# Inverse square roots on VectorE: one second-order and one third-order step in place of three Newton steps

## The chip, the cores and the metric

The kernel runs on one core of a Trainium2 chip. The metric is device time in microseconds (us), the median of three runs. Engine names are those of the profile: PE is TensorE's matmul, PEld its weight load, DVE is VectorE, ACT is ScalarE, POOL is GpSimd and SP is SyncE, which only issues DMAs here.

## The reference

The input x is 4 x 256 rows of 256 float32 numbers. Four layers are added to it in turn, each on a layernorm of x:

```
x = x + tanh(g_xattn[0]) * L0_xattn(layernorm(x), ctx, mask)   # attention, 16 heads; its output is layernormed
x = x + tanh(g_ffn[0])   * L0_ffn(layernorm(x))                # one shared and seven routed experts, top 3
x = x + tanh(g_xattn[1]) * L1_xattn(layernorm(x), ctx, ctx)    # mLSTM cell, 16 heads, each head layernormed
x = x + tanh(g_ffn[1])   * L1_ffn(layernorm(x))                # block-quantised gated FFN, 256 -> 1024 -> 256

_layernorm(x):            (x - m) / sqrt(var + 1e-5)           # over the 256 features
L0_xattn, last line:      (delta - mu) / sqrt(var + 1e-5) * ln_gamma + ln_beta
L1_xattn, each head:      (h - mu) * rsqrt(mean((h - mu)^2) + 1e-6)      # over the head's 16 features
```

## The kernel before, in words

The 1024 rows of x lie in SBUF as eight tiles of 128 rows. Most steps run once for each half, that is for four tiles (n = 0 or 1). One list, `plan`, made by `step_order`, holds the names of all steps; every engine walks through the same list and takes the steps that it has a part in. So the order on each engine is fixed, and the engines meet through semaphores.

The inverse square root is computed by DVE alone, in `inverse_root` (line 1186). It makes a first guess with integer arithmetic on the bits of the float (line 1190) and improves it by three Newton steps of three instructions each (lines 1193, 1195 and 1197). Every one of these ten instructions waits until the one before it has ended: `seq.wait()` waits for the engine's own counter `v_seq`, which each instruction added with `seq.add` raises.

It is called twelve times, with three callers:
- `ln_in(k)`, line 1199, for k = 0 to 7: the statistics of the layernorm of x ahead of each of the four layers, for each half. The operands have 4 columns, one for each tile. `ln_out(k)` then writes the normalised tiles to `tok` (line 1223), which PE transposes (`turn` or `xt`).
- `delta_in(n)`, line 1290: the same for the output of the first attention; 4 columns. `delta_out(n)` adds the result to x.
- `cell_mid(n)`, line 1513: one root for each row and head of the mLSTM cell; 64 columns (4 tiles x 16 heads), in rows of `hstat`, which lies in the memory called `arows` in the profile. `cell_out(n)` uses it.

In the plan the roots stand so: `ln_in(0)` and `ln_in(1)` with the loads and the first transposes; `delta_in(0)` and `ln_in(2)` at the end of the first half's attention; `delta_in(1)` and `ln_in(3)` between the instructions of experts 3 to 5; `ln_in(4)` beside expert 9; `cell_mid(0)` and `ln_in(6)` beside experts 14 and 15; `ln_in(5)` beside the start of the last layer; `cell_mid(1)` and `ln_in(7)` just before the second half of the last layer.

Three other DVE steps are spoken of below. `up` makes the experts' hidden tiles (line 1375), and `accumulate` adds an expert's output to x (line 1386). `quantise` cuts the last layer's operands to blocks; its instructions at lines 1548 and 1550 follow each other with no wait between them. On POOL, `w_split` takes the rounded part off an expert's weights (line 659), and `quantise` hands `mx_grid` to PE (line 584).

Of the kernel before, what the change touches and what calls it, by code (L numbers as in the profile page):

```python
# [36 lines left out]
P = 128  # L37
F32, F32R, BF16, U32, I32, F8 = (mybir.dt.float32, mybir.dt.float32r, mybir.dt.bfloat16, mybir.dt.uint32, mybir.dt.int32,
                                 mybir.dt.float8e4)
ALU = mybir.AluOpType  # L40
# [6 lines left out]
E50, EM50 = float(np.exp(50.0)), float(np.exp(-50.0))  # L47
EXP_BITS = 0x7F800000
FAR = -1e30


class Count:
# [182 lines left out]
def flamingo_layers(nc, a, out):  # L235
# [12 lines left out]
    TH = HALF // P  # L248
# [3 lines left out]
    with ExitStack() as ctx_:  # L252
        place = {}

        def sb(name, shape, dt=F32):
            place[name] = -(-nc.sbuf_base // 32) * 32
            return ctx_.enter_context(nc.sbuf_tensor(name, shape, dt))
# [70 lines left out]
        mv = sb("mv", [P, NT, 2])  # L328
        ve = sb("ve", [P, 8, TH])
        ri = sb("ri", [P, 8, TH])  # L330
        ru = sb("ru", [P, TH])
        dve_ = sb("dve_", [P, 2, TH])
        dri = sb("dri", [P, 2, TH])
        lg = sb("lg", [P, 8, TH, NE])
# [848 lines left out]
        def _(v):  # L1183
            seq = Count(v, s["v_seq"])

            def inverse_root(y, w, u):


                seq.wait()
                seq.add(v.tensor_scalar(y.bitcast(I32), w.bitcast(I32), -0.5, float(0x5F3759DF), ALU.mult, ALU.add))  # L1190
                for _ in range(3):
                    seq.wait()
                    seq.add(v.tensor_tensor(u, y, y, ALU.mult))
                    seq.wait()
                    seq.add(v.scalar_tensor_tensor(u, u, -0.5, w, ALU.mult, ALU.mult))
                    seq.wait()
                    seq.add(v.scalar_tensor_tensor(y, u, 1.5, y, ALU.add, ALU.mult))

            def ln_in(k):

                use, n = k // 2, k % 2
                if use == 0:
                    v.wait_ge(s[f"x_loaded{n}"], 16)
                elif use == 2:
                    v.wait_ge(s["x2_acc"], TH * (NE + 1) * (n + 1))
                i0 = TH * n
                for i in range(i0, i0 + TH):
                    m = seq.add(v.bn_stats(st[:, i, :], x[:, i, :]))  # L1208
                seq.wait(m)
                for i in range(i0, i0 + TH):  # L1210
                    m = seq.add(v.bn_aggr(mv[:, i, :], st[:, i, :]))
                seq.wait(m)
                seq.add(v.tensor_scalar(ve[:, k, :], mv[:, i0:i0 + TH, 1], LN_EPS, None, ALU.add))
                inverse_root(ri[:, k, :], ve[:, k, :], ru[:, :])

            def ln_out(k):
                use, n = k // 2, k % 2
# [72 lines left out]
            def delta_in(n):  # L1290
                i0 = TH * n
                v.wait_ge(s["wo_biased"], 2 * n + 2)
                for i in range(i0, i0 + TH):
                    seq.add(v.bn_stats(st[:, i, :], tok[:, i, :]))
                seq.wait()
                for i in range(i0, i0 + TH):
                    seq.add(v.bn_aggr(mv[:, i, :], st[:, i, :]))
                seq.wait()
                seq.add(v.tensor_scalar(dve_[:, n, :], mv[:, i0:i0 + TH, 1], rs2[:, 1:2], LN_EPS, ALU.mult, ALU.add))
                inverse_root(dri[:, n, :], dve_[:, n, :], ru[:, :])  # L1300
                seq.wait()
                seq.add(v.tensor_scalar(dri[:, n, :], dri[:, n, :], rs2[:, 0:1], None, ALU.mult))

# [209 lines left out]
            def cell_mid(n):  # L1513
                v.wait_ge(s["h_squared"], n + 1)
                seq.add(v.tensor_reduce(hstat[:, 2, n, :], mt[:, :, :].rearrange("p a (h v) -> p (a h) v", v=HD), AX.X, ALU.add))
                seq.wait()
                seq.add(v.tensor_scalar(hstat[:, 3, n, :], hstat[:, 2, n, :], 1.0 / HD, CELL_EPS, ALU.mult, ALU.add))
                inverse_root(hstat[:, 4, n, :], hstat[:, 3, n, :], hstat[:, 5, n, :])

            def cell_out(n):  # L1520
                v.wait_ge(s["h_scaled"], n + 1)
# [82 lines left out]
```

## Time and profile before

| | before |
|---|---|
| median of three runs | 513.97 us |
| the three runs | 513.65, 520.17, 513.97 us |
| span of the profiled execution, first to last instruction | 516.7 us |
| instructions in it | 6750 |
| busy: PE, DVE | 366.7 us (71%), 364.3 us (71%) |
| busy: PEld, ACT, POOL | 247.4, 191.3, 154.6 us |
| mean granted TensorE clock, share of full speed | 0.867 |

The profile is one execution, and it gives no time of its own besides the span. The span counts from the first to the last instruction that the profiler records, and is 2.7 us above the median of the runs. Busy times are sums over the whole span, in which stages with different limits follow one another. In a timeline each line has the start in us, the length in us, the engine, the line of the kernel and what is written from what; the bracket at its end is the idle time of the engine just before it and what ended that.

### The profile page before, as it was taken

The numbers are of one execution on the slowest core, as the hardware profiler recorded it, in microseconds if no ns is written. First come the engines' busy times: TensorE is split into PE (matmuls) and PEld (weight loads), VectorE is DVE, ScalarE is ACT, GpSimd is POOL, SyncE is SP. The second block draws the span as 40 slices with busy tenths as digits, with TensorE's granted clock in tenths as the row PEclk, the third lists the DMA queues.
The fourth block names the chain that finished last, engine by engine and source line by source line (L and its number), as shares of the span: only waits on it lengthen the run. The fifth ranks groups of instructions, "written<-read, shape, count | busy, mean of one in ns | idle before, by whom it ended". The sixth has DMA issues, their size and how long they took to land.

```text
span 516.7 us, 6750 instructions
## 1 busy us (share of the span) xinstructions
PE 366.7 (71%) x2192; PEld 247.4 (48%) x2192; DVE 364.3 (71%) x887; ACT 191.3 (37%) x336; POOL 154.6 (30%) x150
## 2 busy tenths in 40 slices
PE   4664965628998859795975788797686468660665
PEld 2342542405565648584853556565563235530333
DVE  3174875395653498988788656754998697789895
ACT  2333752222441412251334445453201658721231
POOL 5058058100002544554622541212601220030230
PEclk9796997756999998997998899998977879977685
DMA  8499999930111121330498491364100192000001
GB/s 193 134 139 167 148 189 262 266 52 0 42 27 35 62 82 29 94 120 3 119 187 175 92 165 59 59 105 87 18 0 1 47 150 30 2 1 0 20 11 51
DMA packets 47009, 44.20 MB, mean 86 GB/s; under 512 B 6304, under 2 KB 45952, under 8 KB 46976
## 3 DMA queue, kind: packets, MB, share of 16 engines
q1 hardware_dynamic: 44768, 40.53, 38.6%
q0 software_dynamic: 1152, 2.20, 1.8%
q10 hardware_dynamic: 1056, 1.05, 0.7%
q8 instruction: 18, 0.29, 0.3%
q14 instruction: 15, 0.12, 0.1%
HBM read 36.43 MB, written 7.34 MB: 85 GB/s over the span
## 4 chain that ended last, share of the span: by engine, by line
PE 36%; DVE 33%; issue 14%; ACT 7%; DMA 5%; POOL 3%; SPq 1%; DVEq 0%; ACTq 0%; POOLq 0%
PE bank L848 9%; PE bank L874 5%; PE bank L776 4%; DMA probs<-in_L_xattn_Wq 3%; PE bank L733 2%; DVE probs L1264 2%; DVE tok L1223 2%; PE bank L984 2%; PE bank L948 2%; DVE mxraw L1552 2%; DVE mam L1394 2%; DVE probs L1479 1%; PE bank L896 1%; PE bank L810 1%; DVE st L1208 1%
## 5 line engine op out<-in xcount | busy, mean ns | idle before, releaser
L874 PE MATMUL bank<-wexp,wT 128*128 128x256 f32 x192 | 56.1, 420 | 10.1 <-DVE x L1386 10.0
L848 PE MATMUL bank<-tok_r,probs_r 128*128 128x512 f32 x104 | 47.1, 453 | 10.2 <-DVE wT L1375 7.0
L1264 DVE TENSOR_SCALAR probs<-probs,hi 128x512 f32<-128x512 f32 x64 | 32.8, 564 | 28.8 <-ACT probs L1045 28.8
L1097 ACT ACTIVATE silu_sb<-bank 128x512 f32<-128x512 f32 x32 | 19.1, 598 | 86.2 <-PE bank L848 86.2
L659 POOL TENSOR_TENSOR wexp_r<-wexp,probs_r 128x1024 fp32r<-128x1024 f32 x13 | 31.3, 2405 | 58.6 <-ACT probs_r L1056 58.5
L874 PEld LDWEIGHTS bank<-wexp,wT 128*128 128x128 f32 x192 | 38.4, 211 | 17.6 <-issue 12.4
L1045 ACT ACTIVATE probs<-bank 128x1024 f32<-128x1024 f32 x32 | 32.3, 1027 | 38.2 <-PE bank L760 38.2
L584 POOL TENSOR_TENSOR mx_grid<-parts,bl 128x1024 bf16<-128x1024 fp8e4 x9 | 17.2, 1910 | 96.1 <-DVE parts L1555 96.1
L1479 DVE SCALAR_TENSOR_TENSOR probs<-bank,dexp 128x384 f32<-128x384 f32 x48 | 26.5, 555 | 21.7 <-PE bank L934 15.9
L848 PE MATMUL bank<-tok_r,wexp_r 128*128 128x512 f32 x104 | 41.7, 401 | 0.0
L569 POOL TENSOR_TENSOR mxraw<-mxraw,mx_grid 128x512 f32<-128x512 f32 x12 | 15.3, 1275 | 63.8 <-DVE mx_grid L1420 63.8
L1144 ACT ACTIVATE dexp<-bank,geT 128x256 f32<-128x256 f32 x48 | 23.1, 482 | 28.4 <-PE bank L922 28.3
L933 PE MATMUL bank<-qrep,krep 128*128 128x256 bf16 x64 | 18.0, 282 | 17.1 <-DVE probs L1479 13.6
L984 PE MATMUL bank<-ctx,wexp 128*128 128x512 bf16 x64 | 23.5, 529 | 8.4 <-DVE wexp L1564 6.2
L760 PE MATMUL bank<-qrep,krep 128*128 128x256 bf16 x128 | 21.0, 301 | 11.5 <-issue 6.7
L1386 DVE SCALAR_TENSOR_TENSOR x<-bank,cw,x 128x256 f32<-128x256 f32 x64 | 27.4, 476 | 1.6 <-PE bank L874 1.3
L848 PEld LDWEIGHTS bank<-tok_r,probs_r 128*128 128x128 f32 x104 | 20.4, 196 | 16.1 <-DVE wT L1375 7.9
L974 PE MATMUL bank<-identb,mx_grid 128*128 128x128 bf16 x80 | 8.7, 274 | 27.0 <-POOL mx_grid L584 20.6
L776 PE MATMUL bank<-probs,vaug 128*32 128x256 f32 x256 | 18.9, 445 | 9.7 <-DVE probs L1264 9.7
L848 PE MATMUL bank<-xnT_r,probs_r 128*128 128x512 f32 x64 | 25.3, 395 | 0.0
L760 PEld LDWEIGHTS bank<-qrep,krep 128*128 128x128 bf16 x128 | 13.0, 107 | 25.7 <-issue 23.2
L1375 DVE SCALAR_TENSOR_TENSOR wT<-silu_sb,bank 128x512 f32<-128x512 f32 x24 | 16.4, 684 | 12.2 <-ACT silu_sb L1097 6.9
(243 smaller groups left out, 923.0 us busy)
## 6 DMA issues: line engine op xcount, KB each, us to landing
krep<-part_dram SPq DMA_DIRECT2D x64, 128.0 KB, 6.4
qrep<-part_dram SPq DMA_DIRECT2D x64, 128.0 KB, 6.7
wexp<-in_L_ffn_W SPq DMA_DIRECT2D x28, 256.0 KB, 4.4
part_dram<-parts SPq DMA_DIRECT2D x12, 384.0 KB, 3.6
wexp<-in_L_ffn_Wg SPq DMA_DIRECT2D x14, 256.0 KB, 4.4
part_dram<-parts POOLq DMA_DIRECT2D x4, 384.0 KB, 8.1
x<-in_x ACTq DMA_DIRECT2D x2, 512.0 KB, 9.6
ctx<-in_ctx SPq DMA_DIRECT2D x2, 512.0 KB, 9.7
```

The costliest lines, as they stand in the source:

```text
L659: gp.tensor_tensor(low, raw, w_high[k % 2].bitcast(F32), ALU.subtract).then_inc(s["w_low_ready"], 1)
L760: m = pe.matmul(bank[:, bk + hh, S * kc:S * kc + S], krep[:, slot, j, col + P * kc:col + P * kc + P], qrep[:, slot, j, col:col + S], start ...
L776: m = pe.matmul(bank[32 * q:32 * q + 32, 6, S * half:S * half + S], vaug[:, 2 * b + kc, h0:h0 + 32], probs[:, g % 2, j, S * kc:S * kc + S] ...
L848: mm = pe.matmul(bank[:, bk, :], lhs, rhs, start=(kk == 0 and q == 0), stop=(kk == KC - 1 and q == len(terms) - 1))
L874: mm = pe.matmul(bank[:, 2 + pair, D * t:D * t + D], hid[k % 2][m][:, col:col + P], wexp[:, k % WR, 2, m, :], start=(m == 0), stop=(m == 1))
L984: m = pe.matmul(bank[:, 2 * (y % 2) + r, :], xqT[:, k, P * i:P * i + P], wt[:, k, 512 * hf:512 * hf + 512], start=(k == 0), stop=(k == KC ...
L1045: act.activation(probs[:, g % 2, 2 * jj:2 * jj + 2, :], bank[:, bk:bk + 2, :], ACT.Exp, scale=1.0 / float(np.sqrt(HD))).then_inc(s["exp_do ...
L1097: act.activation(silu_sb[:, w % 2, :], bank[:, 0, :], ACT.Silu if direct else ACT.Tanh, scale=1.0 if direct else 0.5).then_inc(s["sigmoid_ ...
L1144: act.activation(dexp_slot(w)[:, 0:S], bank[:, bk, 0:S], ACT.Exp, bias=geT[:, n, 0, 0, row:row + 1]).then_inc(s["d_done"], 1)
L1264: ins = v.tensor_scalar(w, w, hi[:, 2 * b + kc:2 * b + kc + 1], EM50, ALU.min, ALU.max)
L1386: v.scalar_tensor_tensor(x[:, i, :], bank[:, 2 + pair, D * t:D * t + D], cw[:, i, e:e + 1], x[:, i, :], ALU.mult, ALU.add).then_inc(s["x2_ ...
L1479: v.scalar_tensor_tensor(probs[:, g % 2, j, 0:384], bank[:, cell_bank(w)[1], 0:384], 1.0 / float(np.sqrt(HD)), dexp_slot(w), ALU.mult, ALU ...
```

## The change

`inverse_root` gets a fourth argument, a second scratch tile g, and a new body. It starts from another constant, makes one step of second order with a constant fitted to that start, and one step of third order; scale factors are folded into the constants. There are nine instructions. Two of them, those below with no `seq.wait()` ahead, do not wait for the instruction before them. The scratch tile `ru` has two rows in place of one; in `cell_mid` the row 0 of `hstat`, which held sums that have been read by then, serves as g.

```diff
+ROOT_SEED, ROOT_C, ROOT_K = 0x5F370000, 2.989, 0.503195
...
-        ru = sb("ru", [P, TH])
+        ru = sb("ru", [P, 2, TH])
...
-            def inverse_root(y, w, u):
-                seq.wait()
-                seq.add(v.tensor_scalar(y.bitcast(I32), w.bitcast(I32), -0.5, float(0x5F3759DF), ALU.mult, ALU.add))
-                for _ in range(3):
-                    seq.wait()
-                    seq.add(v.tensor_tensor(u, y, y, ALU.mult))
-                    seq.wait()
-                    seq.add(v.scalar_tensor_tensor(u, u, -0.5, w, ALU.mult, ALU.mult))
-                    seq.wait()
-                    seq.add(v.scalar_tensor_tensor(y, u, 1.5, y, ALU.add, ALU.mult))
+            def inverse_root(y, w, u, g):
+                seq.wait()
+                seq.add(v.tensor_scalar(y.bitcast(I32), w.bitcast(I32), -0.5, float(ROOT_SEED), ALU.mult, ALU.add))
+                seq.wait()
+                seq.add(v.tensor_tensor(g, w, y, ALU.mult))
+                seq.wait()
+                seq.add(v.tensor_tensor(u, g, y, ALU.mult))
+                seq.wait()
+                seq.add(v.scalar_tensor_tensor(g, u, ROOT_C, g, ALU.subtract, ALU.mult))
+                seq.add(v.scalar_tensor_tensor(y, u, ROOT_C, y, ALU.subtract, ALU.mult))
+                seq.wait()
+                seq.add(v.tensor_tensor(u, g, y, ALU.mult))
+                seq.wait()
+                seq.add(v.scalar_tensor_tensor(g, u, 10.0 / (3.0 * ROOT_K ** 2), u, ALU.subtract, ALU.mult))
+                seq.add(v.tensor_scalar(y, y, -0.375 * ROOT_K ** 5, None, ALU.mult))
+                seq.wait()
+                seq.add(v.scalar_tensor_tensor(y, g, 5.0 / ROOT_K ** 4, y, ALU.add, ALU.mult))
...
-                inverse_root(ri[:, k, :], ve[:, k, :], ru[:, :])
+                inverse_root(ri[:, k, :], ve[:, k, :], ru[:, 0, :], ru[:, 1, :])
...
-                inverse_root(dri[:, n, :], dve_[:, n, :], ru[:, :])
+                inverse_root(dri[:, n, :], dve_[:, n, :], ru[:, 0, :], ru[:, 1, :])
...
-                inverse_root(hstat[:, 4, n, :], hstat[:, 3, n, :], hstat[:, 5, n, :])
+                inverse_root(hstat[:, 4, n, :], hstat[:, 3, n, :], hstat[:, 5, n, :], hstat[:, 0, n, :])
```

## Rows read from the trace of the kernel before

**Rows 1.** The page: span, the chain by engine, one POOL group.

```profile
span 516.7 us, 6750 instructions
...
PE 36%; DVE 33%; issue 14%; ACT 7%; DMA 5%; POOL 3%; SPq 1%; DVEq 0%; ACTq 0%; POOLq 0%
...
L659 POOL TENSOR_TENSOR wexp_r<-wexp,probs_r 128x1024 fp32r<-128x1024 f32 x13 | 31.3, 2405 | 58.6 <-ACT probs_r L1056 58.5
```

**Rows 2.** The seed's line L1190: duration ns min/median/max, first and last start.

```profile
L1190 DVE TENSOR_SCALAR ri<-ve x8: 170/170/171, 8.6 to 471.5; 128x4 int32<-128x4 int32 x8
L1190 DVE TENSOR_SCALAR dri<-dve_ x2: 170/170/171, 105.1 to 186.1; 128x4 int32<-128x4 int32 x2
L1190 DVE TENSOR_SCALAR arows<-arows x2: 195/195/195, 372.9 to 464.3; 128x64 int32<-128x64 int32 x2
```

**Rows 3.** Timeline of DVE, first delta root: start us, us, instruction.

```profile
105.11 0.17 DVE L1190 TENSOR_SCALAR dri<-dve_ 128x4 int32<-128x4 int32 x1
105.32 0.16 DVE L1193 TENSOR_TENSOR ru<-dri 128x4 f32<-128x4 f32 x1
...
107.09 0.23 DVE L1302 TENSOR_SCALAR dri<-dri,rs 128x4 f32<-128x4 f32 x1
```

**Rows 4.** Timeline of DVE, second cell root.

```profile
464.27 0.20 DVE L1190 TENSOR_SCALAR arows<-arows 128x64 int32<-128x64 int32 x1
...
466.58 0.23 DVE L1197 SCALAR_TENSOR_TENSOR arows<-arows 128x64 f32<-128x64 f32 x1
```

**Rows 5.** Timeline of DVE around instructions that carry no wait for their predecessor.

```profile
375.91 0.23 DVE L1197 SCALAR_TENSOR_TENSOR arows<-arows 128x64 f32<-128x64 f32 x1
376.05 1.65 DVE L1386 SCALAR_TENSOR_TENSOR x<-bank,cw,x 128x256 f32<-128x256 f32 x4
...
384.64 0.69 DVE L1375 SCALAR_TENSOR_TENSOR hid_x<-silu_sb,bank 128x512 f32<-128x512 f32 x1
...
476.57 0.18 DVE L1548 TENSOR_SCALAR bl<-bl 128x32 int32<-128x32 int32 x1
476.66 0.17 DVE L1550 TENSOR_SCALAR bl<-bl 128x32 f32<-128x32 f32 x1
```

**Rows 6.** Timeline of PE at the joins: idle before, and what it waited for.

```profile
117.83 3.64 PE L776 MATMUL bank<-probs,vaug 128*32 128x256 f32 x32 [8.74 <-DVE probs L1264]
...
192.35 1.19 PE L874 MATMUL bank<-wexp,wT 128*128 128x256 f32 x2 [5.33 <-DVE x L1386]
...
219.16 1.09 PE L821 MATMUL bank<-identf,tok 128*128 128x128 f32 x8 [2.49 <-DVE tok L1223]
...
261.90 0.76 PE L821 MATMUL bank<-identf,tok 128*128 128x128 f32 x5 [1.79 <-DVE tok L1223]
...
377.07 1.19 PE L874 MATMUL bank<-wexp,wT 128*128 128x256 f32 x2 [4.69 <-DVE x L1386]
...
480.87 1.03 PE L974 MATMUL bank<-identb,mx_grid 128*128 128x128 bf16 x8 [14.74 <-POOL mx_grid L584]
```

**Rows 7.** Timeline of PE near the other roots.

```profile
16.89 0.92 PE L724 MATMUL bank<-identf,probs 128*128 128x128 f32 x4 [3.55 <-DMA probs<-in_L_xattn_Wq]
...
45.39 1.01 PE L760 MATMUL bank<-qrep,krep 128*128 128x256 bf16 x4 [6.73 <-issue]
...
383.98 0.39 PE L848 MATMUL bank<-tok_r,wexp_r 128*128 128x512 f32 x1
...
397.49 2.21 PE L984 MATMUL bank<-ctx,wexp 128*128 128x512 bf16 x5
399.53 1.04 PE L821 MATMUL bank<-identf,tok 128*128 128x128 f32 x8
```

**Rows 8.** Timeline of POOL and DVE, second delta root.

```profile
187.32 2.34 POOL L659 TENSOR_TENSOR wexp_r<-wexp,probs_r 128x1024 fp32r<-128x1024 f32 x1
...
187.46 2.22 DVE L1197 SCALAR_TENSOR_TENSOR dri<-ru,dri 128x4 f32<-128x4 f32 x1
```

## The prediction

> **What bounds the kernel now.** I read the page first, then the chain of waits in order of time, then the timelines of DVE and PE around each of the twelve roots. By the page no engine is the bound throughout: the chain that ended last lies 36% on PE and 33% on DVE [rows 1], so each stage has to be asked. The seed's line occurs 8, 2 and 2 times [rows 2]; these are the twelve roots, ten with 4 columns and two with 64. In the chain of waits most roots stand whole, instruction by instruction. The second check is PE at the join behind each root: where PE sat idle for longer than the root can shrink, and what ended the idle time comes after the root in DVE's fixed order, a shorter root lets PE start earlier by all that it shrinks.
>
> Nine roots pass it. Both roots of the stretch from 103 to 116 us (the first half's output norm and the next layer's first norm) lie ahead of the clamps for which PE waited 8.74 us. Then come the root of the second half's output norm (PE waited 5.33 us), that of norm 3 (2.49 us), that of norm 4 (1.79 us), the first cell root (4.69 us), and the second cell root and norm 7, in one run of DVE work behind which PE waited 14.74 us [rows 6]. The ninth, norm 6, passes in part, as worked out below.
>
> **What a root costs now.** With 4 columns the seed starts at 105.11, the second instruction at 105.32 and the one behind the tenth at 107.09 [rows 3]. So the seed takes a step of 0.21 us and the nine others 1.77 / 9 = 0.197 us each; the sum is 1.98 us. An instruction is busy for 0.16 to 0.17 of its step, the rest is the hand-over through the semaphore. With 64 columns the seed starts at 464.27 and the tenth instruction at 466.58 [rows 4]: 2.31 us for nine steps. The seed is busy for 0.03 us less than the others there (0.20 against 0.23), so its step is 0.23 and the others' 0.26; the sum is 2.57 us.
>
> **What a root costs after.** Nine instructions, of which seven wait for their predecessor and two do not. The work of each has the forms of before (one or two operands from SBUF, 4 or 64 columns), so the seven keep the steps above. The last of them but one, behind which the final instruction waits, is a multiplication by a constant, the form of the seed, and gets the seed's step. What the two unwaited ones add is not in any root of before. Bounds from the nearest rows: below, the distance at which the engine takes up an instruction that carries no wait, 0.09 us for 32 columns (476.57 to 476.66) and 0.14 us behind one of 64 columns (375.91 to 376.05) [rows 5]; above, a full step, 0.20 or 0.26 us. I take the lower end, 0.09 and 0.14, since these rows show just this case: the second of the two starts while the first is still busy (0.18 and 0.23 us), and only the next waited instruction pays a full step.
> - 4 columns: seed 0.21, five steps of 0.197 = 0.985, one of 0.205, twice 0.09 = 0.18; 1.58 us. Saved: 0.40 us (0.19 with full steps).
> - 64 columns: seed 0.23, five of 0.26 = 1.30, one of 0.23, twice 0.14 = 0.28; 2.04 us. Saved: 0.53 us (0.29 with full steps).
>
> The Trainium skill ("VectorE: DVE Perf Modes", section "The DRAIN you can't avoid") says that the next operation does not start until the pipe has emptied and that leaving out semaphores gains nothing; by that both unwaited instructions would cost full steps. The trace disagrees, by the 0.09 us at 476.57; the same section allows an earlier start to an operation that isn't held.
>
> **What of it lies on the path.**
> - Six roots with 4 columns pass whole: both of 103 to 116 us, the second output norm, norms 3, 4 and 7. 6 x 0.40 = 2.4 us.
> - The two cell roots: 2 x 0.53 = 1.06 us.
> - Norm 6: what follows its root on DVE is the hidden tile at 384.64 [rows 5], which also needs PE's product. The last matmul of that starts at 383.98 and lasts 0.39 us, to 384.37 [rows 7]. DVE could come 0.40 us earlier but finds its data only 0.27 us earlier. Less the hand-over, 0.25 us.
> - Norm 0: nothing. PE turns the weights first, and waited 3.55 us more for Wq's DMA, to 16.89 [rows 7], long after the root (seed at 8.6 [rows 2]). If that cover went, it would be worth 0.40.
> - Norm 1: nothing. PE and ACT finish with its tiles and then PE waits 6.73 us, to 45.39, for the stacked copies of k and q [rows 7]. Their stores were issued from splits that DVE makes ahead of this root. Cover gone: 0.40.
> - Norm 5: nothing. PE works at the last layer's products until it takes up the transposes of this norm at 399.53 without a gap [rows 7]. A shorter root only adds to that cover.
>
> Sum: 2.4 + 1.06 + 0.25 = 3.7 us. Against the profiled execution: 516.7 - 3.7 = 513.0 us of span. That execution stands 2.7 us above the median of the runs, whose difference I take over: 513.97 - 3.7 = **510.3 us**.
>
> The other edits cost nothing. The second scratch row and row 0 of the head statistics are written and read by DVE alone, in order, and the sums in that row were read two steps of the plan before. No wait, DMA or PSUM bank is added, nothing is queued behind a new wait, and POOL's and SP's queues hold what they held. Between the joins the savings travel through stretches bound by PE, ACT or a DMA round trip; those start on what the shorter chain delivers, so they shift and do not absorb, as far as the chain of waits shows.
>
> **Rivals.**
> *A, no overlap.* The unwaited instructions cost full steps; only one instruction in ten is saved. 6 x 0.19 + 2 x 0.29 + 0.19 = 1.9 us, so 512.1 us. Against it stand the pairs of rows 5; for it, that in none of them do both members work in place on scratch tiles with two inputs from SBUF, as the first new pair does.
>
> *B, given back.* DVE gets ahead, but some join waits for something that does not move, such as a weight's DMA or a POOL subtraction, and the gain ends there. What certainly reaches the end is the last run (cell root and norm 7, 0.53 + 0.40 = 0.93 us): 513.0 us, and 514.0 if nothing does. For it: the chain crosses DMAs (5%) and 14% "issue", in which the profile names no releaser [rows 1]. Against it: PE's gaps of 1.79 to 14.74 us behind DVE [rows 6].
>
> *C, slower, by POOL's subtractions.* POOL's L659, 13 of them at 2.4 us each [rows 1], holds DVE up: the one at 187.32 lasted 2.34 us, and a DVE instruction that started at 187.46 took 2.22 us in place of 0.16, so to POOL's end [rows 8]. Such a stall costs 2.06 us. If the new phase puts more DVE chains of experts 3 to 15 behind the start of an L659, each adds up to that. It decides from 3.7 / 2.06 = 1.8 new stalls: two give 510.3 + 4.1 = 514.4, three 516.5 us. For it: the new root still has nine instructions of the kinds that were held there. Against it: L659 is released by ACT, which follows PE, which follows the same DVE chain, so most phases move together; and a shift of 0.4 us is small beside 2.3. The Trainium skill ("SBUF — State Buffer", section "Who interferes with whom") says that DVE with two SBUF inputs and GpSimd share a port pair as an exclusive lock, first come first served; the 2.22 us agree.
>
> *D, more.* The stall of rows 8 disappears by the same shift (2.06 us more), or the covered roots count too, 3 x 0.40 and the rest of norm 6, 0.15: 510.3 - 1.35 = 508.9, with the stall gone as well 506.9 us.
>
> **How the numbers follow.** Forecast, 509.3 to 511.5: 0.60. A: 0.10. B: 0.12. C: 0.12. D: 0.06. The range goes from 508.0, inside D, to 514.3, where C begins; it leaves out C, half of D, and a rest for a median that falls on an execution like the 520.17 one. A measurement of this kernel tells about 2% from no change, here 10.3 us, so beyond 503.7 or 524.3. All twelve roots at their full gain give 5.1 us, and five new stalls would be needed for the other side. Faster by over 2%: 0.02, within: 0.95, slower: 0.03.
>
> **What would show it.** In the profile after: a root with 4 columns takes 1.58 us from its seed to what follows, one with 64 columns 2.04 us; its fifth and its eighth instruction start 0.09 to 0.14 us behind the fourth and the seventh, overlapping them (if 0.20 or 0.26, A). DVE has 12 instructions fewer. PE's waits at the joins of rows 6 stay within 0.5 us of before, each join some 0.4 to 0.5 us further ahead than the last, 3.7 us in all at the end (if the lead stops growing or falls back at one of them, B, and the wait there names the culprit). DVE instructions that last some 2 us beside an L659: one in the roots, as before (if several new ones, C). The forecast is wrong if steps of waited instructions change with the new forms, or if the lead at 480 us is under 2 us.

## The result

The changed kernel takes 516.09 us (median of 20 runs, 510.90 to 520.70), the kernel before 518.19 us (median of 20 runs, 513.65 to 521.39, the three of before among them). The ratio is 0.9937, with a 95% interval of 0.9912 to 0.9963: 3.3 us less, at least 1.9 and at most 4.6. That is no change by the measure of 2%, and a small gain by the interval. The plain medians differ by 2.1 us. The ratio and its interval leave out the executions that took over 1.5% longer than the fastest of the same kernel, three of the changed kernel and one of before; with all forty in, the means differ by 2.2 us. The profiled execution of the changed kernel took 515.3 us with a span of 513.2 us, at a mean granted clock of 0.877; its span is 3.5 us shorter than that of before [rows 1]. Each span is one execution of a kernel whose times spread over 8 to 10 us, so this difference shows nothing by itself.

The forecast of 510.3 us was wrong, and 516.09 us lies outside its range of 508.0 to 514.3. The gain was forecast as 3.7 us and the comparison finds 3.3; what failed is the time from which it was taken off.

From the page of the changed kernel: the span, the busy times by engine, the chain by engine, and the POOL group that rival C speaks of (now L660).

```profile
span 513.2 us, 6734 instructions
...
PE 367.6 (72%) x2188; PEld 248.2 (48%) x2192; DVE 360.7 (70%) x875; ACT 191.5 (37%) x336; POOL 154.5 (30%) x150
...
PE 36%; DVE 33%; issue 14%; ACT 7%; DMA 6%; POOL 3%; SPq 2%; DVEq 0%; ACTq 0%; POOLq 0%
...
L660 POOL TENSOR_TENSOR wexp_r<-wexp,probs_r 128x1024 fp32r<-128x1024 f32 x13 | 31.3, 2405 | 57.3 <-ACT probs_r L1057 57.2
```

DVE has 875 instructions where it had 887, twelve fewer, one in each root, and is busy for 3.6 us less. The chain has the same shares to within 1% of the span [rows 1]: no new bound has come up.

Timeline of DVE in the changed kernel, three roots: the first delta root, the second delta root as far as its stalls, and the second cell root. Columns as in [rows 3].

```profile
105.12 0.17 DVE L1193 TENSOR_SCALAR dri<-dve_ 128x4 int32<-128x4 int32 x1
...
105.72 0.16 DVE L1199 SCALAR_TENSOR_TENSOR ru<-ru 128x4 f32<-128x4 f32 x1
105.80 0.15 DVE L1200 SCALAR_TENSOR_TENSOR dri<-ru,dri 128x4 f32<-128x4 f32 x1
...
106.19 0.16 DVE L1204 SCALAR_TENSOR_TENSOR ru<-ru 128x4 f32<-128x4 f32 x1
106.27 0.17 DVE L1205 TENSOR_SCALAR dri<-dri 128x4 f32<-128x4 f32 x1
...
106.67 0.23 DVE L1312 TENSOR_SCALAR dri<-dri,rs 128x4 f32<-128x4 f32 x1
...
185.09 0.89 DVE L1195 TENSOR_TENSOR ru<-dve_,dri 128x4 f32<-128x4 f32 x1
...
186.21 2.23 DVE L1199 SCALAR_TENSOR_TENSOR ru<-ru 128x4 f32<-128x4 f32 x1
...
462.10 0.20 DVE L1193 TENSOR_SCALAR arows<-arows 128x64 int32<-128x64 int32 x1
...
462.85 0.23 DVE L1199 SCALAR_TENSOR_TENSOR arows<-arows 128x64 f32<-128x64 f32 x1
462.99 0.22 DVE L1200 SCALAR_TENSOR_TENSOR arows<-arows 128x64 f32<-128x64 f32 x1
...
463.87 0.23 DVE L1207 SCALAR_TENSOR_TENSOR arows<-arows 128x64 f32<-128x64 f32 x1
```

The root with 4 columns takes 106.67 - 105.12 = 1.55 us; before it took 1.98 [rows 3]. Its two unwaited instructions start 0.08 us behind their partners, while those are still busy, where a waited one starts 0.197 us behind. With 64 columns the last instruction starts 1.77 us after the seed, and with its own step of 0.26 us the root takes 2.03 us, against 2.57 [rows 4]; the unwaited ones start 0.14 us behind. In the second delta root one instruction is held for 2.23 us beside POOL's subtraction, as one was before [rows 8]; the shorter stall at 185.09 (0.89 us) stood there before too, with 0.90 us.

Timeline of PE in the changed kernel, the joins that answer to [rows 6] and, first, the scores of [rows 7].

```profile
46.63 1.86 PE L761 MATMUL bank<-qrep,krep 128*128 128x256 bf16 x8 [8.74 <-issue]
...
116.97 3.64 PE L777 MATMUL bank<-probs,vaug 128*32 128x256 f32 x32 [7.23 <-DVE probs L1274]
...
190.37 1.19 PE L875 MATMUL bank<-wexp,wT 128*128 128x256 f32 x2 [4.59 <-DVE x L1396]
...
216.84 1.97 PE L822 MATMUL bank<-identf,tok 128*128 128x128 f32 x8 [2.49 <-DVE tok L1233]
...
260.02 1.10 PE L822 MATMUL bank<-identf,tok 128*128 128x128 f32 x8 [1.35 <-DVE tok L1233]
...
373.82 3.64 PE L875 MATMUL bank<-wexp,wT 128*128 128x256 f32 x8 [4.32 <-DVE x L1396]
...
477.72 1.04 PE L975 MATMUL bank<-identb,mx_grid 128*128 128x128 bf16 x8 [13.54 <-POOL mx_grid L585]
```

Against [rows 6] the joins from 116.97 on come 0.86, 1.98, 2.32, 1.88, 3.25 and 3.15 us earlier, and the end 3.5. The lead grows, but not by 0.4 to 0.5 us from one to the next. Two leads were won and lost before 104 us: Wq's DMA came 0.5 us earlier, and the stacked copies of k and q 1.2 us later (46.63 against 45.39 [rows 7]). At 216.84 PE's eight transposes last 1.97 us, against 1.09 before: the granted clock from 216 to 221 us was 0.66, where it was 1.00 before, and the lead fell from 2.32 to 1.00 us at PE's next wait, behind 236 us. Such things move single joins by up to 1.3 us in either direction; a lead at one join can't be read as a sum of roots. PE's waits at these joins, which I had expected within 0.5 us of before, moved more too: 8.74 us became 7.23, and 14.74 became 13.54.

To get round that, I measured intervals between two points of DVE's own work. Such a point is the instruction that merges a norm's statistics (BATCH_NORM_AGGREGATE in the profile). From that of the first delta root to that of norm 2, DVE waits for no other engine: 7.77 us before, 7.35 after (-0.42, one root). From norm 6's to norm 5's, a stretch with one root in it and no idle time of DVE in either profile: 12.91 before, 12.47 after (-0.44). The three long and noisy intervals are given as before and after. They hold the first layer's attention and DMAs (28 to 104 us: 75.89 and 76.24), the stretch from norm 4 to norm 6 (124.38 and 122.58), and that from norm 5 to norm 7 (75.79 and 76.76).

### The profile page after: what moved, and what is told of

Same layout as the page of the kernel before. It is cut to its first block, busy times and chain, and to the rows that moved or that the text cites. A ratio compares the mean times of both kernels' runs of the same rounds, so it can differ in the third digit from the quotient of the medians.

```text
span 513.2 us, 6734 instructions
## 1 busy us (share of the span) xinstructions
PE 367.6 (72%) x2188; PEld 248.2 (48%) x2192; DVE 360.7 (70%) x875; ACT 191.5 (37%) x336; POOL 154.5 (30%) x150
## 4 chain that ended last, share of the span: by engine, by line
PE 36%; DVE 33%; issue 14%; ACT 7%; DMA 6%; POOL 3%; SPq 2%; DVEq 0%; ACTq 0%; POOLq 0%
PE bank L849 10%; PE bank L875 5%; PE bank L777 4%; DVE probs L1274 3%; DMA probs<-in_L_xattn_Wq 3%; PE bank L949 2%; PE bank L985 2%; DVE mxraw L1562 2%; DVE tok L1233 2%; DVE mam L1404 2%; PE bank L734 2%; DVE probs L1489 2%; DMA krep<-part_dram 1%; PE bank L897 1%; PE bank L761 1%
## 5 line engine op out<-in xcount | busy, mean ns | idle before, releaser
L660 POOL TENSOR_TENSOR wexp_r<-wexp,probs_r 128x1024 fp32r<-128x1024 f32 x13 | 31.3, 2405 | 57.3 <-ACT probs_r L1057 57.2
```

The lines of the kernel that those rows point to most:

```text
L660: gp.tensor_tensor(low, raw, w_high[k % 2].bitcast(F32), ALU.subtract).then_inc(s["w_low_ready"], 1)
```

## The experiments

Eleven runs in three groups, three of them of a kernel that had been run already. Each group is on one chip with its own runs of the kernel before: 519.82 us (median of 29, 514.44 to 523.65) for the first four, 518.08 us (17 runs, 514.88 to 522.52) for the next four, 518.96 us (21 runs, 512.53 to 520.47) for the last three. The profiles of the first two are of executions with spans of 520.0 and 519.6 us, at the long end of their spread, so only their DVE steps are used, not their spans.

**The changed kernel again.** No edit.

> The changed kernel once more, beside the kernel before on the same chip. Theory (nine roots on the path, 0.4 to 0.5 us each): 3.7 us less than the kernel before of the same call, a ratio of 0.993, whatever the level at which both run. Rival 'given back': 0 to 0.9 us less, a ratio of 0.998 to 1.000. Rival 'all twelve roots count': 5.1 us less, 0.990. If the absolute time of the kernel before again spreads over 513 to 521 us, my base of 513.97 us, a median of three, was the low end of that spread and not the kernel's level.

Measured: 516.92 us (12 runs), ratio 0.9939 (0.9900 to 0.9979). On another chip the gain is the same, 3.2 us of 519.82.

**Waits put ahead of the two unwaited instructions.** In the changed kernel:

```
                 seq.add(v.scalar_tensor_tensor(g, u, ROOT_C, g, ALU.subtract, ALU.mult))
+                seq.wait()
                 seq.add(v.scalar_tensor_tensor(y, u, ROOT_C, y, ALU.subtract, ALU.mult))
...
                 seq.add(v.scalar_tensor_tensor(g, u, 10.0 / (3.0 * ROOT_K ** 2), u, ALU.subtract, ALU.mult))
+                seq.wait()
                 seq.add(v.tensor_scalar(y, y, -0.375 * ROOT_K ** 5, None, ALU.mult))
```

> The changed kernel with a wait put ahead of each of the two instructions that had none (nine steps in line). Theory: each such instruction costs a full step in place of 0.08 or 0.14 us, so a root with 4 columns takes 1.55 + 2 x 0.12 = 1.79 us and one with 64 columns 2.03 + 2 x 0.12 = 2.27 us; 1.9 us over the nine roots, so 1.8 us less than the kernel before (0.9965). Rival (the overlap of the pairs is worth nothing, as when the pipe had to empty anyway): the same time as the changed kernel, 0.993.

Measured: 517.8 us (12 runs), ratio 0.9945 (0.9906 to 0.9984). The interval holds both expected ratios, so the time tells nothing. The DVE timeline of this kernel, first delta root, does:

```profile
109.12 0.17 DVE L1193 TENSOR_SCALAR dri<-dve_ 128x4 int32<-128x4 int32 x1
...
109.72 0.16 DVE L1199 SCALAR_TENSOR_TENSOR ru<-ru 128x4 f32<-128x4 f32 x1
109.92 0.16 DVE L1201 SCALAR_TENSOR_TENSOR dri<-ru,dri 128x4 f32<-128x4 f32 x1
...
110.31 0.16 DVE L1205 SCALAR_TENSOR_TENSOR ru<-ru 128x4 f32<-128x4 f32 x1
110.50 0.17 DVE L1207 TENSOR_SCALAR dri<-dri 128x4 f32<-128x4 f32 x1
...
110.91 0.23 DVE L1314 TENSOR_SCALAR dri<-dri,rs 128x4 f32<-128x4 f32 x1
```

With the waits the partners start 0.20 and 0.19 us behind instead of 0.08, and the root takes 1.79 us instead of 1.55. The two intervals of DVE's chain say the same: 7.57 and 12.73 us, against 7.35 and 12.47. So of the 0.42 us that a root saves, more than half (0.22 to 0.26) comes from the two starts without a wait and the rest from the instruction that is gone.

**The first guess alone, in all twelve roots.** In the kernel before:

```
-                for _ in range(3):
+                for _ in range(0):
```

> The kernel before with the nine improving instructions left out of every root, so that only the first guess is used: the same cut at the same places, four times as large. Six roots of 4 columns at 1.77 us, two of 64 columns at 2.33 us, and 0.25 us for norm 6 with its cap. Theory: 10.6 + 4.7 + 0.25 = 15.5 us less than before, 0.970. Rival 'all twelve roots count': 10 x 1.77 + 4.7 = 22.4 us, 0.957. Rival 'given back at joins': under half of 15.5 us, over 0.985.

Measured: 500.18 us (6 runs), ratio 0.9614 (0.9561 to 0.9667), so 20.1 us less. What the roots shed is not given back: had the gain ended at a join that does not move, it would have stayed at a few us. It is more than the 0.970 of the sum by path. Part of that is norm 6: its interval falls from 12.91 to 11.16 us, 1.75 us, a whole root, where I had allowed 0.25. (With the roots of the next run but one it is 12.18 us; see there.) The rest is taken up with the run of the nine roots below.

**The first guess alone in norms 0, 1 and 5**, the three that I called covered. In the kernel before:

```
-            def inverse_root(y, w, u):
+            def inverse_root(y, w, u, steps=3):
...
-                for _ in range(3):
+                for _ in range(steps):
...
-                inverse_root(ri[:, k, :], ve[:, k, :], ru[:, :])
+                inverse_root(ri[:, k, :], ve[:, k, :], ru[:, :], 0 if k in (0, 1, 5) else 3)
```

> The kernel before with the nine improving instructions left out in norms 0, 1 and 5 alone, the three roots that I called covered. Theory: no change, 1.000 (within 0.002). Rival 'all twelve roots count': 3 x 1.77 = 5.3 us less, 0.990.

Measured: 518.42 us (12 runs), ratio 0.9975 (0.9942 to 1.0008). Three roots cut to their first guess, 5.3 us of DVE time, buy nothing that can be told from zero, and 0.990 is excluded. The timeline of PE in this kernel, around norm 1:

```profile
32.25 1.95 PE L733 MATMUL bank<-ctxT,wT 128*128 128x512 f32 x4 [0.82 <-ACT wT L1018]
...
45.41 1.87 PE L760 MATMUL bank<-qrep,krep 128*128 128x256 bf16 x8 [9.49 <-issue]
```

PE waits 0.38 us for the norm in place of 2.15, comes to the scores earlier and sits idle ahead of them for 9.49 us in place of 6.73, until 45.41 us in place of 45.39 [rows 7]. So something that this root does not move hides it. I took it for the round trip of the copies; the profile names nothing there ("issue"), and the run with six steps in norm 1, below, puts that in doubt.

**The first guess alone in the nine others.** The same edit with `3 if k in (0, 1, 5) else 0`, and 0 for the delta and cell roots.

> The kernel before with the nine improving instructions left out of the nine roots that I called exposed, and kept in norms 0, 1 and 5. The cut in all twelve took 20 us (0.9614, 0.956 to 0.967), more than the 15.5 of my sum. Theory (the surplus comes from the exposed roots, above all from the second half's output norm, whose nine left-out instructions held two stalls behind POOL worth 2.8 us, and from norm 6 without its cap, 1.5 us): the same as with all twelve, 0.961 to 0.965. Rival (the three covered roots gave the surplus, 5.3 us): 0.971 to 0.974.

Measured: 498.81 us (6 runs), ratio 0.9623 (0.9575 to 0.9671), 19.5 us less. The nine alone give as much as all twelve, within the intervals, so the surplus over 15.5 us is not the covered three's. The sum of the nine by their steps is 7 x 1.77 + 2 x 2.31 = 17.0 us with norm 6 whole; 2.5 us are left. The timeline of this kernel's DVE and POOL around the second delta root and norm 3 shows where a surplus comes up; the last line stands behind norm 6's root:

```profile
183.18 0.17 DVE L1190 TENSOR_SCALAR dri<-dve_ 128x4 int32<-128x4 int32 x1
183.39 0.90 DVE L1302 TENSOR_SCALAR dri<-dri,rs 128x4 f32<-128x4 f32 x1
184.20 1.65 DVE L1386 SCALAR_TENSOR_TENSOR x<-bank,cw,x 128x256 f32<-128x256 f32 x4
...
184.38 2.36 POOL L659 TENSOR_TENSOR wexp_r<-wexp,probs_r 128x1024 fp32r<-128x1024 f32 x1
...
195.78 0.69 DVE L1375 SCALAR_TENSOR_TENSOR wT<-silu_sb,bank 128x512 f32<-128x512 f32 x1 [0.24 <-issue]
...
198.23 1.38 DVE L1213 TENSOR_SCALAR ve<-mv 128x4 f32<-128x4 f32 x1
...
367.91 0.69 DVE L1375 SCALAR_TENSOR_TENSOR hid_x<-silu_sb,bank 128x512 f32<-128x512 f32 x1 [0.96 <-PE bank L848]
```

Of the kernel before, timeline of DVE, the lines that answer to those at 195.78 and 198.23:

```profile
204.70 0.69 DVE L1375 SCALAR_TENSOR_TENSOR wT<-silu_sb,bank 128x512 f32<-128x512 f32 x1 [1.93 <-ACT silu_sb L1097]
...
207.15 0.17 DVE L1213 TENSOR_SCALAR ve<-mv 128x4 f32<-128x4 f32 x1
```

The root is over when POOL's subtraction starts, DVE is by then at an instruction that reads a PSUM bank, and that takes 1.65 us, no longer than elsewhere: the 2.06 us of stall [rows 8] are gone. DVE's wait of 1.93 us for ACT is 0.24 us here. Against that, the first instruction of norm 3 is now held beside POOL, for 1.38 us in place of 0.17. 2.06 + 1.69 - 1.21 = 2.5 us. The signs and the places are in the run with all twelve as well (178.80, 193.68 us). That the sum comes out even is not to be trusted: it takes norm 6 whole, and in this profile it isn't. DVE is done with norm 6's first guess and then waits 0.96 us for PE's product (367.91), so the interval from norm 6 to norm 5 is 12.18 us, only 0.73 less than before. Measured by the same points, the stretch from the second delta root to norm 4 takes 71.6 to 72.5 us in the five profiles in which its two roots are those of before, 65.5 us here and 65.7 with all twelve cut: 5.9 to 7.0 us less, of which the two roots are 3.5. So the stretch that gives the surplus, some 2.4 to 3.5 us, is the same in both profiles; the three terms are one reading of it.

**Six Newton steps in place of three, in all twelve roots.** In the kernel before, `range(6)`.

> The kernel before with six Newton steps in place of three, in all twelve roots: nine more instructions in each. Theory: seven roots of 4 columns at 1.77 us (norm 6 too, since a longer chain has no cap), two of 64 columns at 2.31 us, and norm 5, whose thin cover the longer root outlasts, by about 1.4 us; norms 0 and 1 stay covered. 12.4 + 4.6 + 1.4 = 18.4 us more, 1.0355. Rival 'all twelve count': 22.3 us, 1.043. Rival 'given back at joins': under half, below 1.018.

Measured: 541.74 us (6 runs), ratio 1.0426 (1.0386 to 1.0466), 22.1 us more (20.0 to 24.1). The point by path, 1.0355, is missed, and that of all twelve, 1.043, is met. Longer roots are not the mirror of shorter ones. The timeline of PE in this kernel:

```profile
417.63 1.97 PE L821 MATMUL bank<-identf,tok 128*128 128x128 f32 x8 [1.54 <-DVE tok L1223]
...
507.34 1.03 PE L974 MATMUL bank<-identb,mx_grid 128*128 128x128 bf16 x8 [18.80 <-POOL mx_grid L584]
```

At 417.63 PE waits 1.54 us for norm 5, for which it did not wait before (399.53 in [rows 7]): its cover was thinner than 1.77 us. And behind that wait the transposes last 1.97 us in place of 1.04. The windows of this kernel ahead of and behind norm 5's transposes (window, its length, busy time and count of PE, PEld, DVE, ACT and POOL, granted clock, DMA share, GB/s):

```profile
412.00:417.00 5.00, 3.19 (x7) 1.04 (x8) 4.20 (x26) 1.64 (x3) 0.00 (x0) 0.50 0.00 0
417.00:425.00 8.00, 6.68 (x32) 3.61 (x34) 1.77 (x4) 3.51 (x5) 2.92 (x3) 0.50 0.01 2
```

The windows of the kernel before over the same matmuls:

```profile
394.00:399.00 5.00, 3.80 (x15) 1.81 (x16) 4.48 (x23) 1.62 (x2) 0.03 (x1) 0.50 0.00 0
399.00:406.00 7.00, 5.21 (x42) 2.81 (x40) 2.33 (x6) 3.89 (x6) 2.93 (x3) 0.97 0.01 2
```

In both kernels the granted clock stood at 0.50, its lower level of 1.2 GHz, ahead of these transposes; before it had risen by the time that PE ran them and the gate's matmuls (0.97), and here it stayed at 0.50. From the start of norm 5's transposes to the last group of the gate's matmuls it is 425.36 - 417.63 = 7.73 us here and 403.97 - 399.53 = 4.44 us in the kernel before: 3.3 us more for the same work. Over the eleven profiles in which PE does not wait there it is 4.44 to 5.21 us, because the clock rises at different moments (in the changed kernel the transposes take 1.91 us with no wait ahead), so the wait goes with 2.5 to 3.3 us more. 17.0 us for the nine roots, 1.5 of waiting and 2.5 to 3.3 of lower clock make 21.0 to 21.8 us, and 22.1 were measured (20.0 to 24.1). Whether the wait brings the lower clock, and whether norm 1 comes out from under its cover too, is asked by two kernels further on.

**A cheaper second step.** If more than half of the gain lies in unwaited starts and missing steps, a chain shorter still should give more. In the changed kernel the second step is one of second order with its factor formed beside the product:

```
                 seq.add(v.tensor_tensor(u, g, y, ALU.mult))
-                seq.wait()
-                seq.add(v.scalar_tensor_tensor(g, u, 10.0 / (3.0 * ROOT_K ** 2), u, ALU.subtract, ALU.mult))
-                seq.add(v.tensor_scalar(y, y, -0.375 * ROOT_K ** 5, None, ALU.mult))
-                seq.wait()
-                seq.add(v.scalar_tensor_tensor(y, g, 5.0 / ROOT_K ** 4, y, ALU.add, ALU.mult))
+                seq.add(v.tensor_scalar(h, y, 0.5 * ROOT_K ** 3, None, ALU.mult))
+                seq.wait()
+                seq.add(v.scalar_tensor_tensor(y, u, 3.0 / ROOT_K ** 2, h, ALU.subtract, ALU.mult))
```

`h` is a third scratch row (row 1 of the head statistics in the cell). The root's relative error, worked out in float32, is 1.3e-6 at most, against under 3e-7 in the changed kernel and 1.6e-7 before.

> The changed kernel with a second step of second order in place of the one of third order: eight instructions, two of them unwaited, six steps in line (error of the root 1.3e-6 in place of 2.7e-7). Theory: a root with 4 columns takes 0.205 + 5 x 0.197 + 2 x 0.08 = 1.35 us, one with 64 columns 1.78 us; against the kernel before 7 x 0.63 + 2 x 0.79 = 6.0 us less, 0.9885, and some 2 us less than the changed kernel. Rival (the gain saturates, since engines other than DVE are reached at the joins): as the changed kernel, 0.993 to 0.994.

Measured: 512.47 us (6 runs, 509.19 to 514.15), ratio 0.9850 (0.9809 to 0.9891), 7.8 us less than before (5.6 to 9.9). It is faster than both kernels: its interval ends below that of the changed kernel (0.9912 and up), though the two ratios are from different chips. The DVE timeline of this kernel, first delta root:

```profile
108.66 0.17 DVE L1189 TENSOR_SCALAR dri<-dve_ 128x4 int32<-128x4 int32 x1
...
109.53 0.16 DVE L1198 TENSOR_TENSOR ru<-ru,dri 128x4 f32<-128x4 f32 x1
109.61 0.16 DVE L1199 TENSOR_SCALAR ru<-dri 128x4 f32<-128x4 f32 x1
109.80 0.16 DVE L1201 SCALAR_TENSOR_TENSOR dri<-ru 128x4 f32<-128x4 f32 x1
110.00 0.23 DVE L1306 TENSOR_SCALAR dri<-dri,rs 128x4 f32<-128x4 f32 x1
```

1.34 us, 0.64 less than before; the intervals are 7.13 and 12.27 us (-0.64 each).

**The kernel before, unchanged**, as a control.

> The kernel before, under a label of its own, as a control. All theories: 1.000. What it tells: how far from 1 a ratio of this kernel comes out in five rounds when nothing is changed, whether its times spread over 513 to 521 us, and by its profile in which stretches two executions of the same program differ. If the stretches from 28 to 104 us and from 258 to 382 us (by the statistics of the norms) differ by several us while the runs of DVE work at 104 to 112 and at the end agree to 0.1 us, the level of the runs is set there, by clock and transfers, and not by the roots.

Measured: 518.88 us (12 runs, 512.43 to 521.81), ratio 0.9982 (0.9942 to 1.0022). Its profile (span 516.8 us) repeats the two intervals of DVE's own chain to 0.01 us and the rest not. The intervals of these and other kernels, in us:

```
                      first delta   norm 6 to   norm 1 to     norm 4 to   norm 5 to   span
                      to norm 2     norm 5      first delta   norm 6      norm 7
before                  7.77          12.91       75.89        124.38       75.79     516.7
before again            7.77          12.92       77.39        123.26       78.02     516.8
changed                 7.35          12.47       76.24        122.58       76.76     513.2
two second-order        7.13          12.27       79.25        122.17       74.56     512.1
guess alone, all        6.00          11.16       74.05        124.17       75.05     497.3
guess alone, nine       6.00          12.18       77.47        118.29       73.32     494.9
six steps, all          9.76          14.68       77.88        130.13       83.82     541.5
```

The first two columns follow the roots' length to 0.02 us, with two exceptions: the first with six steps (1.99 us longer for 1.77), and the second with the guess alone in nine roots, where DVE waits for PE's product. The next three differ by 1.1 to 2.2 us between the two executions of one and the same program (before and before again).

**Six Newton steps in norm 5 alone.** The edit of the covered roots, with `6 if k == 5 else 3`.

> The kernel before with six Newton steps in the root of norm 5 alone, 1.77 us more DVE time at one place. In the run with six steps everywhere PE waited 1.54 us for this norm, and behind that wait its transposes and three groups of the gate's matmuls took 1.82 to 1.97 us each in place of 1.03 to 1.06 (granted clock 0.50 for 0.97). Theory, the wait itself brings the lower clock: a wait of 1.4 to 1.7 us in front of norm 5's transposes, behind it two or more gate groups near 1.9 us, so 1.5 + 3.3 = 4.8 us at the gate's last group; ratio 1.009, 522.5 us against 518. Rival, the clock there had fallen for another reason (other landings, longer roots ahead): the same wait, but gate groups at 1.03 to 1.06 us as in the nine profiles without a wait; 1.5 us, ratio 1.003.

Measured: 522.66 us (10 runs), ratio 1.0091 (1.0046 to 1.0136), 4.7 us more (2.4 to 7.1) for 1.77 us of DVE time under a cover; 1.003 is excluded. The timeline of PE in this kernel:

```profile
401.77 1.09 PE L821 MATMUL bank<-identf,tok 128*128 128x128 f32 x8 [1.62 <-DVE tok L1223]
403.60 1.92 PE L896 MATMUL bank<-xnT,wgate 128*32 128x256 f32 x8 [0.74 <-ACT xnT L1083]
405.31 1.75 PE L896 MATMUL bank<-ctxT,wgate 128*32 128x256 f32 x8
406.89 1.03 PE L896 MATMUL bank<-xnT,wgate 128*32 128x256 f32 x8
407.76 1.03 PE L896 MATMUL bank<-ctxT,wgate 128*32 128x256 f32 x8
```

The wait is 1.62 us and two of the gate's four groups take 1.92 and 1.75 us. In the eleven profiles in which PE does not wait there, all four take 1.03 to 1.06. Here the clock had risen ahead of the transposes (1.00 from 400 to 403 us) and fell again behind them (0.57 from 403 to 407), where in the run with six steps everywhere it had not risen yet. Since this kernel differs from the one before in one root only, the wait and the slower groups both come from the longer root, and the time says that it costs more than its 1.77 us. That it is the wait which holds the clock down, and not the later arrival in some other way, is what the two traces suggest; no run separates them. From the transposes to the last group it is 5.99 us, against 4.44 to 5.21 without a wait: 0.8 to 1.55 us more, so 2.4 to 3.2 us are seen at this place, and the rest of the 4.7 lies inside the interval.

**Six Newton steps in norm 1 alone.** The same edit with `6 if k == 1 else 3`.

> The kernel before with six Newton steps in the root of norm 1 alone. PE already waits 2.15 us for this norm, so PE comes 1.77 us later to the transposes (a wait near 3.9 us). Theory, the round trip of the stacked copies hides it, since their stores are issued from work ahead of this root: the stores at 40.3 us and the first scores at 44.9 to 45.4 us, as in the profiles of before; ratio 1.000. Rival, the cover is thin for a longer root, as at norm 5: stores up to 1.8 us later (42.19 was seen with six steps everywhere), scores 0.9 to 1.8 us later, ratio 1.002 to 1.0035. The time alone can hardly tell them apart; the start of the stores and of the scores does.

Measured: 518.95 us (12 runs), ratio 1.0009 (0.9983 to 1.0035). By the time the cover holds. By the traces the reason that I gave for it is wrong in part. The SP queue's entry for the stores, and PE's first scores, in this kernel:

```profile
43.01 2.23 SPq L478 DMA_DIRECT2D part_dram<-parts  x2
...
46.35 1.87 PE L760 MATMUL bank<-qrep,krep 128*128 128x256 bf16 x8 [4.87 <-issue]
```

The stores come 2.7 us later than the 40.28 of before, so they do follow norm 1. The scores follow the stores only loosely. In six of the thirteen profiles the pairs of store and scores are 36.60 and 44.22 (guess alone, all), 37.54 and 45.41 (covered three), 38.81 and 44.94 (control), 39.82 and 47.09 (two second-order steps), 42.19 and 46.27 (six, all), 43.01 and 46.35 here. With all thirteen, stores before 39 us go with scores at 44.2 to 45.4, and later ones with 45.4 to 47.1 in no order.

**The cheaper second step again.** No edit against that kernel.

> The changed kernel with the cheaper second step, unchanged, on another chip. By its roots it gains 7 x 0.64 + 2 x 0.80 = 6.1 us, ratio 0.988; the first measurement said 7.8 us, ratio 0.985. If the surplus of 1.7 us is real, the ratio is again near 0.985; if it was chance, 0.988 or a little above. Above 0.992 the roots' sum itself would be wrong. The interval of DVE's chain from the first delta root to norm 2 should be 7.13 us again.

Measured: 512.40 us (6 runs, 509.43 to 513.71), ratio 0.9878 (0.9833 to 0.9923), 6.3 us less. The interval from the first delta root to norm 2 is 7.14 us. The roots' sum of 6.1 us lies in both intervals (5.6 to 9.9 and 4.0 to 8.7), so no surplus over it is shown; nor is one excluded, since 7.8 lies in both too.

## Why the prediction was wrong, by its own steps

**The base: this step failed.** The prediction said that the profiled execution "stands 2.7 us above the median of the runs, whose difference I take over: 513.97 - 3.7". Two errors lie in it. First, it set a span beside a time. In every execution for which both are known, the time is 2.0 to 2.2 us more than the span (515.3 and 513.2, 499.38 and 497.3, 518.84 and 516.8), so the profiled execution of before, of span 516.7, took some 518.8 us. Second, it took 513.97 for the kernel's level. The three runs were 513.65, 520.17 and 513.97; twenty gave 518.19, other runs 519.82 (29) and 518.08 (17). 513.97 was the low end of a spread of 8 us, and the profiled execution an ordinary one. The first error moves nothing in the sum, since 516.7 - 2.7 is 513.97 again; it hid that the profiled execution stood 4.8 us above that median and not 2.7. The second moved the forecast by 518.19 - 513.97 = 4.2 us. The three runs already spread over 6.5 us, almost twice the gain. From the level of the twenty runs the same sum gives 518.19 - 3.7 = 514.5 us, 1.6 below the measured 516.09, and from the profiled execution's own time 518.8 - 3.7 = 515.1. And the range, 6.3 us wide, was built of the doubts about the gain, with only "a rest" for a median near 520: it had to carry the doubt about the level, which was the larger.

**What a root costs before and after: right.** 1.58 and 2.04 us were forecast, 1.55 and 2.03 measured; of the 0.03 us, 0.01 for each unwaited start (0.08 for 0.09) is 0.02. The control repeats 1.98.

**No overlap (rival A): did not happen.** The partners start 0.08 and 0.14 us behind. With waits they start 0.20 us behind, and the root is 0.24 us longer in the timeline. The Trainium skill ("VectorE: DVE Perf Modes", section "The DRAIN you can't avoid") says that the next operation does not start until the pipe has emptied and that a semaphore cost nothing beside that in its measurement of copies; for instructions of 4 columns the two kernels' timelines disagree, by 0.12 us for each wait. The same section lets an operation that is not held start earlier, and with that the 0.08 us agree.

**What lies on the path: right for the eight whole roots as a sum (none was changed alone); norm 6's cap is real, but its 0.25 us was one execution's.** The interval of norm 6 gave 0.44 us in the changed kernel and 1.75 with the guess alone in all twelve, and lost 1.77 with six steps: a whole root each time. With the guess alone in nine roots it gave 0.73, and DVE's wait of 0.96 us for PE's product (367.91) is just the cap that I had named. What I took as fixed was when that product ends. In the profile of before it ends 1.59 us behind the start of the seed; in the control, the same program, 0.44 us behind it; in the changed kernel 0.66; with the guess alone in all twelve 0.98 us ahead of it. In the profile of before the matmuls on the way to it still took 0.61 to 0.63 us each at 381 us, in the control 0.39 to 0.40. So the root counts whole in some executions and in part in others, and the sum lies between 3.7 and 3.9 us. Measured: 3.3, with 1.9 to 4.6 as its interval. The runs cannot tell 3.7 from 3.9, nor either from the 2.2 us by which the means of all runs differ.

**Norms 0, 1 and 5 count nothing: right for a shorter root.** Taking nearly all of them away gave a ratio of 0.9975 with 1.000 in its interval, and the nine others alone gave what the twelve gave (19.5 and 20.1 us). The cover of norm 5 is thin in the other direction: with 1.77 us more, PE waits 1.5 to 1.6 us there, the gate's matmuls behind it run at the lower clock, and alone it costs 4.7 us (2.4 to 7.1). The prediction said that a shorter root "only adds to that cover", and asked nothing of a thinner one. Norm 1's cover was argued from stores issued ahead of its root; they are issued behind it (43.01 us with six steps there), and what sets the start of the scores is not found.

**Given back (rival B): did not happen.** Of the 17.0 us that the guess-alone kernels take out of the nine roots nothing is missing at the end, where 19.5 and 20.1 us arrive (2.4 to 3.5 of them a surplus of the stretch with POOL's stall). The lead at 480 us, for which under 2 us would have meant a wrong forecast, was 3.15. But the sign that I named, joins each 0.4 to 0.5 us further ahead, is not one that a single trace can give: clock and DMA landings moved leads by up to 1.3 us.

**Slower by POOL's subtractions (rival C): did not happen.** The second delta root has its one long stall, 2.23 us at 186.21, where it had 2.22 [rows 8]. The one new long instruction in a root, the seed of the first cell root with 1.09 us, stands beside another POOL instruction (L576) and takes the place of one of 0.95 us. POOL's group is unchanged, 13 of 2405 ns. The Trainium skill ("SBUF — State Buffer", section "Who interferes with whom") speaks of an exclusive lock on a port pair, for DVE instructions with two SBUF inputs beside GpSimd; the 2.23 us agree, of an instruction of that form. The 1.65 us at 184.20 show that one which reads a PSUM bank is not held beside such a subtraction.

**More (rival D): its stall goes, but not by 0.4 us.** The rest of norm 6, 0.15 us, did come in the changed kernel's profile. The stall stayed where it was. Roots shorter by 1.77 us end before the subtraction starts, and then its 2.06 us are gone; a new stall of 1.2 us comes up behind it. Both were read from the traces of two kernels; no run moved the subtraction alone. The covered roots, D's other half, count nothing that can be told from zero.

**Left open:** what sets the start of the first scores (44.2 to 47.1 us over the profiles), which hides the root of norm 1; and whether the subtraction alone, moved by 0.4 us with the roots unchanged, would take the stall with it.

## What to carry to other kernels

Before a gain of a few us is taken off a time, ask how far the runs of the unchanged kernel lie apart: three runs that spread over 6.5 us do not give a level to 3 us, and the span of a profiled execution has to be set against that execution's own time. A chain of small dependent VectorE instructions is priced by its number of waited steps more than by its work (0.197 us a step with 4 columns, 0.26 with 64), and an independent instruction put in without a wait costs about half a step (0.08 and 0.14 us); whether it reaches the end is asked at the join behind it, by what the other engine waits for there. A small gain is then shown in an interval that holds DVE's chain alone, where one execution repeats the last to 0.01 us, not in the span. And where two engines meet at one tile, look at a second execution before the slack is given a number: here it was 0.27 us in one and 1.4 us in the next of the same program.

## What the runs showed that I had not expected

- The same program, run again and again on one chip, spreads over 9 us (514.44 to 523.65). Its DVE chains repeat to 0.01 us (7.77 and 7.77, 12.91 and 12.92); the three long stretches between other norms differ by 1.1 to 2.2 us each.
- A VectorE instruction of 4 columns with no wait starts 0.08 us behind one that is busy for 0.16 us, one of 64 columns 0.14 us behind one of 0.23. A wait for the predecessor makes it 0.197 and 0.26.
- Small shifts of the same work go with another granted clock: at one join of the changed kernel transposes of 1.09 us took 1.97 (0.66 from 216 to 221 us, where it had been 1.00). In two runs of two, a new wait of 1.5 to 1.6 us was followed by 0.8 to 3.3 us more at a granted clock near 0.50, and a root longer by 1.77 us at that place alone cost 4.7 us (2.4 to 7.1): a cover that runs out can cost more than what it is short of.
